# Moving most transposes of a fused LoRA MLP from TensorE to VectorE, and the mixing product to an earlier place

## The reference, cut to what matters

```python
x = x + conv(x) * mask                        # stage 0: long convolution by a state space kernel
x = x + einsum('bct,bcd->bdt', x, W1[cond])   # stages 1 and 2: a 32 x 32 matrix for each sample
x = x + einsum('bct,bcd->bdt', x, W2[cond])
# stage 3: gated MLP, H = 512, F = 1376, with one of 16 adapters (rank 16) for each sample
gate = x @ W_gate.T + 0.5 * (x @ A_gate[r].T) @ B_gate[r].T
up   = x @ W_up.T   + 0.5 * (x @ A_up[r].T)   @ B_up[r].T
act  = silu(gate) * up
x = x + act @ W_down.T + 0.5 * (act @ A_down[r].T) @ B_down[r].T
```

## Time and profile before

| | |
|---|---|
| median of 3 runs | 1069.36 us (1068.21 to 1069.70) |
| the profiled execution, its own time | 1069.72 us |
| its span, first to last instruction | 1067.9 us |
| TensorE busy, mean granted clock | 97%, 0.997 |
| VectorE, ScalarE, GpSimd busy | 46%, 38%, 45% |
| DMA engines busy (main queue) | 41.3% |

### The profile page before, as it was taken

The page is one execution under the profiler, slowest core; times in us unless marked ns, Lnnn a source line. Parts: engine busy times, 40 slices in busy tenths (PEclk is TensorE's granted clock), DMA queues, the critical chain, the costliest instruction groups (busy, mean ns, idle before and its releaser), DMA issues.

```text
span 1067.9 us, 19023 instructions
## 1 busy us (share of the span) xinstructions
PE 1037.9 (97%) x5922; PEld 906.3 (85%) x5922; DVE 490.4 (46%) x1095; ACT 402.1 (38%) x627; POOL 484.8 (45%) x301
## 2 busy tenths in 40 slices
PE   3999899999999999999999999999999999999998
PEld 3665688888898888888888988888888888888887
DVE  8333344545444445445454445454454444454442
ACT  7002234434433433344343334334443433443341
POOL 0605354545445444545454454445454544544441
PEclk9999899999999999999999999999999999999999
DMA  9799342424333343424243333434242433334320
GB/s 340 249 404 337 116 110 89 134 69 138 98 109 101 99 123 101 120 84 136 71 138 97 108 99 101 125 99 122 80 137 73 137 96 107 102 98 128 104 75 20
DMA packets 100980, 135.50 MB, mean 127 GB/s; under 512 B 26395, under 2 KB 59420, under 8 KB 100956
## 3 DMA queue, kind: packets, MB, share of 16 engines
q1 hardware_dynamic: 100380, 135.12, 41.3%
q10 hardware_dynamic: 576, 0.08, 0.1%
HBM read 118.11 MB, written 16.99 MB: 127 GB/s over the span
## 4 chain that ended last, share of the span: by engine, by line
PE 94%; DVE 3%; DMA 3%; issue 0%; ACT 0%; DVEq 0%; ACTq 0%
PE ps L984 47%; PE ps L1016 27%; PE ps L994 8%; PE ps L962 5%; PE ps L1005 4%; DMA x1p<-yo 2%; PE ps L1039 1%; PE ps L1038 1%; PE ps L975 1%; PE ps L972 1%; PE ps L973 1%; DVE x3r L815 0%; DMA tr<-kpad 0%; DVE xs L704 0%; PE ps L936 0%; PE ps L1027 0%
## 5 line engine op out<-in xcount | busy, mean ns | idle before, releaser
L984 PE MATMUL ps<-wg_hi,x_hi 128*128 128x512 f32 (+2 forms) x768 | 299.2, 390 | 4.6 <-DVE x_lo L805 4.6
L984 PE MATMUL ps<-wg_lo,x_hi 128*128 128x512 f32 (+2 forms) x768 | 291.7, 380 | 0.0
L984 PE MATMUL ps<-wg_hi,x_lo 128*128 128x512 f32 (+2 forms) x768 | 290.7, 379 | 0.0
L471 POOL TENSOR_TENSOR bst<-braw,bst 128x1024 fp32r<-128x1024 f32 (+1 forms) x96 | 212.7, 2215 | 90.7 <-ACT bst L572 90.7
L815 DVE STREAM_TRANSPOSE x3r<-x3n 32x128 f32<-32x128 f32 x512 | 155.0, 303 | 92.3 <-ACT x3n L545 85.8
L588 ACT ACTIVATE at_hi<-ps 128x512 fp32r<-128x512 f32 (+1 forms) x95 | 53.4, 562 | 315.1 <-PE ps L1005 315.1
L984 PEld LDWEIGHTS ps<-wg_hi,x_hi 128*128 128x128 f32 x768 | 145.1, 189 | 25.9 <-issue 4.7
L984 PEld LDWEIGHTS ps<-wg_hi,x_lo 128*128 128x128 f32 x768 | 145.1, 189 | 25.2
L984 PEld LDWEIGHTS ps<-wg_lo,x_hi 128*128 128x128 f32 x768 | 145.3, 189 | 20.4
L1016 PE MATMUL ps<-wd_hi,at_hi 128*128 128x288 f32 x696 | 151.9, 300 | 0.0
L1016 PE MATMUL ps<-wd_lo,at_hi 128*128 128x288 f32 x696 | 149.0, 296 | 0.0
(11 more groups left out here) (147 smaller groups left out, 1184.6 us busy)
## 6 DMA issues: line engine op xcount, KB each, us to landing
braw<-in_tb SPq DMA_DIRECT2D x256, 128.0 KB, 2.7
braw<-in_tb SPq DMA_DIRECT2D x128, 96.0 KB, 2.4
adraw<-in_tad SPq DMA_DIRECT2D x128, 88.0 KB, 1.9
tr<-kpad SPq DMA_DIRECT2D x16, 512.0 KB, 6.9
x1p<-yo SPq DMA_DIRECT2D x16, 512.0 KB, 5.7
xb<-in_x SPq DMA_DIRECT2D x32, 256.0 KB, 2.8
agraw<-in_ta SPq DMA_DIRECT2D x128, 64.0 KB, 2.0
bdraw<-in_tbd SPq DMA_DIRECT2D x128, 64.0 KB, 2.2
```

The lines of the kernel that those rows point to most:

```text
L471: sub(v, b_from(p, q), v.bitcast(F32), ALU.subtract).then_inc(s["blo"], 1)
L984: last = mm(bank[:, 0:n], x3s[a][:, k, :], wgs[b][:, k, o:o + n], start=(k == 0 and a + b == 0), stop=False, skip_group_check=True)
```

## The change

- VectorE makes the transposes of groups 1 and 2 (`a_turn` in the VectorE list, 16 instructions each, from `act_t` into `atp`). TensorE keeps those of group 0, and group 2 of the last tile.
- x3 is turned from a new SBUF copy `x3m` back into the PSUM bank `misc`, in two halves, and `x3_high` and `x3_low` read it there. A new ScalarE copy `x3_keep` saves x3 in `x3n` for the final sum. `x3r` goes away.
- On TensorE `mix(t + 1)` moves from behind `chunk(p, 2, 0)` to behind `chunk(p, 0, 1)`; `chunk(p, 1, 0)` moves ahead of `lora_b(t, p, 0)`, and `down` of group 2 behind it.
- `x` rows and mix weights are loaded for tile t + 2 in tile t; those of tile 1 are loaded ahead of the first block. The adapter loads for the next tile come first in `tile_io`. `x1_high` and `x1_low` come earlier in their lists.
- New semaphores: `atv` (VectorE turned a group), `dn` (`down` of group 0 or 1 is done), `x3k` (x3 saved).

```diff
 def x3_copy(t):                      # ScalarE
     act.wait_ge(s["x3mm"], t + 1)
-    copy(x3n[:, p, :], misc, ACT.Copy).then_inc(s["x3n"], 1)
+    copy(x3m[:], misc, ACT.Copy).then_inc(s["x3n"], 1)
+def x3_keep(t, p, free=None):
+    act.wait_ge(s["x3n"], t + 1)
+    if free is not None:
+        act.wait_ge(s["evac"], free)
+    copy(x3n[:, p, :], x3m[:], ACT.Copy).then_inc(s["x3k"], 1)
...
 def a_high(t, q, to=None):
-    act.wait_ge(s["att"], t * 3 + q + 1)
+    if q == 0:
+        act.wait_ge(s["att"], t + 1)
+    elif to is not None:
+        act.wait_ge(s["att"], NT + 1)
+    else:
+        act.wait_ge(s["dn"], t * 2 + q)
+        act.wait_ge(s["atv"], t * 2 + q)
...
+def turn(to, of, blocks):             # VectorE
+    for i, j in blocks:
+        rows, cols = slice(i * C, (i + 1) * C), slice(j * C, (j + 1) * C)
+        last = V.transpose(to[cols].rearrange("f (k n) -> f k n", n=P)[:, :, rows],
+                           of[rows].rearrange("n (k f) -> n k f", f=P)[:, :, cols])
+    return last
+GRID = [(i, j) for i in range(GB) for j in range(GB)]
+def x3_turn(t, part, done=False):
+    dve.wait_ge(s["x3n"], t + 1)
+    last = turn(misc, x3m[:], part)
+    if done:
+        last.then_inc(s["x3t"], 1)
+def a_turn(t, q):
+    dve.wait_ge(s["mul"], t * 3 + q + 1)
+    turn(atp, act_t[:], GRID).then_inc(s["atv"], 1)
...
 # tile_dve
 act_mul(t - 1, 1 - p, 2)
+a_turn(t - 1, 2)
 t_mask(t, p); t_turn(t); a_low(t - 1, 2); t_low(t)
-td_mask(t - 1, 1 - p); td_turn(t - 1)
+x3_turn(t + 1, GRID[0:8])
 act_mul(t, p, 0)
+x3_turn(t + 1, GRID[8:16], True)
+td_mask(t - 1, 1 - p); td_turn(t - 1)
+a_low(t, 0)
 td_low(t - 1)
-a_low(t, 0)
 out_sum(t - 1, ...)
 act_mul(t, p, 1)
-x3_turn(t + 1, 1 - p)
+a_turn(t, 1)
 a_low(t, 1); x3_low(t + 1)
...
 # tile_pe
 chunk(p, 0, 0)
-a_turn(t - 1, 2)
 chunk(p, 0, 1)
-down(t - 1, 1 - p, 2)
+mix(t + 1, 1 - p)
+pe.wait_ge(s["mul"], t * 3)
+chunk(p, 1, 0)
 lora_b(t, p, 0)
-chunk(p, 1, 0)
+down(t - 1, 1 - p, 2)
 a_turn(t, 0); chunk(p, 1, 1); lora_b_down(t - 1, 1 - p); lora_b(t, p, 1); chunk(p, 2, 0)
-mix(t + 1, 1 - p)
 down(t, p, 0)
-a_turn(t, 1)
 chunk(p, 2, 1); lora_b(t, p, 2); down(t, p, 1)
...
 # tile_act
 silu(t - 1, 1 - p, 2)
+x1_high(t + 1)
 a_high(t - 1, 2); t_high(t)
+x3_copy(t + 1)
 b_high(t, p, 1); silu(t, p, 0)
-td_high(t - 1); a_high(t, 0); ag_high(t + 1); x1_high(t + 1)
+ag_high(t + 1); a_high(t, 0); td_high(t - 1)
 b_high(t, p, 2); silu(t, p, 1); bd_high(t)
-x3_copy(t + 1, 1 - p); a_high(t, 1)
+x3_keep(t + 1, 1 - p)
 ad_high(t + 1); b_high(t + 1, 1 - p, 0)
+a_high(t, 1)
 x3_high(t + 1)
...
 # tile_io (SP queue)
-load_x(t + 1); load_b(t, here, p, 2)
-load_ag(t + 1); load_ad(t + 1); load_wbd(t, mixes, 1 - p); load_b(t + 1, there, 1 - p, 0)
+load_ag(t + 1); load_ad(t + 1); load_b(t, here, p, 2); load_b(t + 1, there, 1 - p, 0)
+mix_data(t + 2, mixes, p)             # load_x(t + 2), load_wbd(t + 2)
 store_out(t - 1); load_b(t + 1, there, 1 - p, 1); load_bd(t + 1)
```

More of the change, by code:

```diff
@@ L169, in cond_resid_kernel @@
         x3s = [sb("x3_hi", [P, KT, TN], F32R), sb("x3_lo", [P, KT, TN], F32R)]
-        x3r = sb("x3r", [P, T])
+        x3m = sb("x3m", [P, T])
         act_t = sb("act_t", [P, T])
@@ L185, in cond_resid_kernel @@
             ag aghi aglo ad adhi adlo b0 b1 bhi blo bd bdhi bdlo
-            bfree la tm tmt thi2 tlo2 gu silu mul att ahi alo td tdm tdt tdhi tdlo accd evac ost""".split() + [
+            bfree la tm tmt thi2 tlo2 x3k gu silu mul att atv dn ahi alo td tdm tdt tdhi tdlo accd evac ost""".split() + [
             f"wl{n}" for n in range(NW)] + [f"u{q}" for q in range(C // 2)]
@@ L338, in store_out, with mix_data @@
                 sp.dma_start(out[bass.ds(row, TN), :], outb[:]).then_inc(s["ost"], 16)
+            def mix_data(t, e, p):
+                load_x(t)
+                load_wbd(t - 1, e, p)
             def tile_io(t, p, here, there, mixes, first=False, last=False):
-                if not last:
-                    load_x(t + 1)
-                load_b(t, here, p, 2, t * 3 + 1)
                 if not last:
@@ L346, in tile_io @@
                     load_ad(t + 1, there)
-                    load_wbd(t if not first else None, mixes, 1 - p)
+                load_b(t, here, p, 2, t * 3 + 1)
+                if not last:
                     load_b(t + 1, there, 1 - p, 0, t * 3 + 2)
+                if mixes is not None:
+                    mix_data(t + 2, mixes, p)
                 if not first:
@@ L357, in block_io @@
                 there = None if last else entries(SP, i + 1, 0, NA, 0, GB)
-                mixes = entries(SP, i, 1, NCOND, GB, BB)
-                after = None if last else entries(SP, i + 1, 1, NCOND, 0, GB)
+                mixes = None if last else entries(SP, i + 1, 1, NCOND, 0, BB)
                 if first:
                     load_b(0, here[0:GB], 0, 1)
-                tile_io(i * 2, 0, here[0:GB], here[GB:], mixes, first=first)
-                tile_io(i * 2 + 1, 1, here[GB:], there, after, last=last)
+                tile_io(i * 2, 0, here[0:GB], here[GB:], None if last else mixes[0:GB], first=first)
+                tile_io(i * 2 + 1, 1, here[GB:], there, None if last else mixes[GB:], last=last)
             sp.wait_ge(s["kout"], 32)
@@ L423, in _ @@
             sp.wait_ge(s["yst1"], 16 * C // 4)
+            load_wbd(None, entries(SP, 0, 1, NCOND, GB, BB), 1)
+            load_x(1)
             block_io(0, first=True)
@@ L483, in tile_lows @@
                     x_sum(t + 1)
+                    x1_low(t + 1)
                 b_low(t, p, 1)
@@ L486, in tile_lows @@
                     ag_low(t + 1)
-                    x1_low(t + 1)
                 b_low(t, p, 2)
@@ L541, in x1_high, with x3_copy @@
                 copy(x1_hi[:], xa[:], ACT.Copy).then_inc(s["x1hi"], 1)
-            def x3_copy(t, p):
+            def x3_copy(t):
                 act.wait_ge(s["x3mm"], t + 1)
-                copy(x3n[:, p, :], misc, ACT.Copy).then_inc(s["x3n"], 1)
+                copy(x3m[:], misc, ACT.Copy).then_inc(s["x3n"], 1)
[4 more added lines that the diff above has]
+                copy(x3n[:, p, :], x3m[:], ACT.Copy).then_inc(s["x3k"], 1)
             def x3_high(t, free=None):
@@ L550, in x3_high @@
                     act.wait_ge(s["gu"], free)
-                copy(x3s[0][:].rearrange("p k n -> p (k n)"), x3r[:], ACT.Copy).then_inc(s["x3hi"], 1)
+                copy(x3s[0][:].rearrange("p k n -> p (k n)"), misc, ACT.Copy).then_inc(s["x3hi"], 1)
             def ag_high(t, first=False):
@@ L603, in _ @@
             act.wait_ge(s["yst1"], 16 * C // 4)
-            x3_copy(0, 0)
+            x3_copy(0)
             x3_high(0)
+            x3_keep(0, 0)
             act.wait_ge(s["msk"], 1)
@@ L611, in tile_act @@
                     silu(t - 1, 1 - p, 2)
+                if not last:
+                    x1_high(t + 1)
+                if not first:
                     a_high(t - 1, 2)
                 t_high(t)
+                if not last:
+                    x3_copy(t + 1)
                 b_high(t, p, 1, None if first else t * 3)
                 silu(t, p, 0)
+                if not last:
+                    ag_high(t + 1)
+                a_high(t, 0)
                 if not first:
                     td_high(t - 1)
[L618 to L621, removed]
                 b_high(t, p, 2, t * 3 + 1)
@@ L625, in tile_act @@
                 if not last:
-                    x3_copy(t + 1, 1 - p)
+                    x3_keep(t + 1, 1 - p, None if first else t)
+                    ad_high(t + 1, 1 - p, None if first else t)
+                    b_high(t + 1, 1 - p, 0, t * 3 + 2)
                 a_high(t, 1)
                 if not last:
-                    ad_high(t + 1, 1 - p, None if first else t)
-                    b_high(t + 1, 1 - p, 0, t * 3 + 2)
                     x3_high(t + 1, t * 3 + 3)
@@ L804, in x3_low @@
                 dve.wait_ge(s["x3hi"], t + 1)
-                tt(x3s[1][:].rearrange("p k n -> p (k n)"), x3r[:], x3s[0][:].rearrange("p k n -> p (k n)").bitcast(F32),
+                tt(x3s[1][:].rearrange("p k n -> p (k n)"), misc, x3s[0][:].rearrange("p k n -> p (k n)").bitcast(F32),
                    ALU.subtract).then_inc(s["x3lo"], 1)
-            def x3_turn(t, p):
-                dve.wait_ge(s["x3n"], t + 1)
[L811 to L816, removed]
+            def turn(to, of, blocks):
[6 more added lines that the diff above has]
+            def x3_turn(t, part, done=False):
+                dve.wait_ge(s["x3n"], t + 1)
+                last = turn(misc, x3m[:], part)
[4 more added lines that the diff above has]
+                turn(atp, act_t[:], GRID).then_inc(s["atv"], 1)
             def t_mask(t, p):
@@ L863, in out_sum @@
                 dve.wait_ge(s["accd"], t + 1)
+                dve.wait_ge(s["x3k"], t + 1)
                 if stored is not None:
@@ L875, in _ @@
             tt(x1_lo[:], xa[:], x1_hi[:].bitcast(F32), ALU.subtract).then_inc(s["x1lo"], 1)
-            x3_turn(0, 0)
```

(29 more changed lines are left out.)

## The result

The median went from 1069.31 us (4 executions, 1068.21 to 1069.70) to 1039.26 (4 executions, 1037.27 to 1040.91): ratio 0.972, interval 0.970 to 0.974. A ratio is the time over that of the kernel before; an interval is one of 95%. A later set of 5 on chip 0 gave 1038.70, ratio 0.970 (0.969 to 0.971). The forecast was 1036, its range 1031 to 1052.

A forecast was written before the change was run, and what follows sets the result against it. TensorE's instruction stream was taken as the bound, 29.40 us a tile. Savings of 33.0 in tiles 1 to 30 plus 0.88 in the last, less 0.6 in tile 0, made 33.3: 1036 us, range 1031 to 1052.

The forecast's parts named there:

- The path: TensorE, steady tiles: two groups of transposes at 0.44 us and a 0.22 us wait go, 1.10 a tile, 33.0 in all.
- The last tile's 0.88: TensorE, last tile: it loses its two groups of four transposes, 0.88 us; its tail stays as before.
- The price of a turn into PSUM: VectorE's transposes writing PSUM instead of SBUF: extra cost taken as 0, at most 0.133 us a turn.
- rival 1: VectorE turns into PSUM cost 0.054 to 0.10 us more each: 1043 us at 0.065, 1051 at 0.08; chance 0.12.
- the walk's tightest place: Rows laid end to end: group 1's low part ready at 24.2, due at TensorE's `down` at 25.1, 0.87 us to spare.
- The due times: Steady tile, all engines: each result for TensorE comes before it is wanted, so the tile takes 28.3 us.
- rival 2: VectorE's turns become the bound, over 0.10 us dearer each: 1117 us at 0.133; chance 0.08.
- Rival 3: The early `mix` on TensorE waits for its x: half a microsecond a tile gives 1052 us; chance 0.05.
- Rival 4: The transposes' time on TensorE comes back as other gaps, so nothing moves: 1069 us; chance 0.02.
- Tile 0: the mis-sized term: SP queue in tile 0: loads and index reads ahead of B delay it; charged 0.6 us, between 0 and 4.
- The median: Whole kernel: 1036.4 us from the profiled execution's 1069.72, taken as 1036 since the median was 0.4 lower.
- `x3_low`: VectorE subtraction: falls from 2.13 to about 0.69 us, taking an operand from PSUM.

The follow-up runs named there:

- Experiment 1: Changed kernel with group 1's four transposes back on TensorE, behind `down` of group 0: 1052.93 us, ratio 0.983 to the kernel before.
- experiment 2: Kernel before with the 16 turns of x3 cut in two halves, `a_low` of group 1 between them: 1064.26 us, ratio 0.994.
- experiment 3: Changed kernel with two or six further unused VectorE turns before those of group 1: 1046.78 us (ratio 0.980) and 1086.71 us (1.016).
- Experiment 8: Changed kernel with group 0's transposes on VectorE too, second half of x3's turns behind the final sum: 1130.15 us, ratio 1.055.
- experiment 5: Changed kernel with x and mix weights loaded one tile ahead again, at the head of a tile's loads: 1122.96 us, ratio 1.050.
- Experiment 6: Changed kernel with the loads around tile 0 reordered, B of groups 1 and 2 earlier: 1036.48 us and again 1036.37, ratio 0.967 both times.
- experiment 4: Changed kernel with x3 turned into an SBUF tensor instead of the PSUM bank `misc`: 1038.02 us, ratio 0.971.

## Why the prediction was right

**The path.** The step that carried the forecast, 1.10 us a tile from two groups of 0.44 and a wait of 0.22, measured 1.130. Experiment 1 put one of the groups back and found 0.440; experiment 2 took the wait out alone and found 0.217; the other group wasn't tested by itself. The last tile's 0.88 came out as 0.9.

**The price of a turn into PSUM.** Taken as 0, with 0.133 as the upper bound; it is 0.020. The page "Perfetto Trace Analysis" of the Trainium skill, section "Optimizing Scalar/DVE Operations", puts VectorE's access to PSUM (125 ns) 65 ns above that to SBUF (60 ns); the turns show 21 ns (0.324 against 0.303 us into SBUF in the kernel before). At 0.020 the price is below the 0.054 at which, by the prediction, it begins to count, so rival 1 didn't happen. Of the 0.87 us to spare 0.55 is left, and 16 × 0.020 is 0.32: the walk's tightest place was the right one. What it left out is that the weight loads want `at_lo` earlier: 0.39 of the 0.55 is free (experiment 3). So the price begins to count at about 0.044, an estimate by (0.87 − 0.16) / 16, and 0.020 is below that too.

**The due times.** No steady tile has a wait. Experiment 3 shows the cliff at the place that the walk named: past 0.39 us every added one counts (no dose below 0.61 was run). Experiment 8 gives rival 2 in another form: with 16 more turns the round through `td_low` and `lora_b_down` is the bound. Rival 3 came only with the late load of experiment 5. Rival 4 fell with the result, and experiment 1 shows that the transposes' time on TensorE counts in full.

**Tile 0: the mis-sized term.** It was charged 0.6 us and measured 2.6, and 0.3 ahead of it from the 16 dearer turns. The step was named (B of group 2 late by the loads and index reads put in front), and its bounds of 0 and 4 hold it. The walk had B of group 2 land at 137.7; it landed at 139.5. The four A issues behind the index reads took 3.55 us, against 1.99 in the kernel before, and the walk as recorded doesn't name the 1.3 us that ScalarE spends on a table load before its first silu (in both kernels). Experiment 6 gets 1.2 us back.

**The median.** 1036 against 1039.26. The 3.3 us are a sum in which errors partly cancel. Tile 0 and its lead cost 2.3 more than charged, the steady tiles gave 0.9 more than forecast (33.9 for 33.0): 1.4 by the profiled executions, 1037.8 against 1036.4. The other 1.9 us is how those executions lie to their medians, 0.4 above before and 1.5 below after. That the changed kernel's median lies higher comes from the two executions at 0.993; the trace of experiment 4 shows such a loss ahead of the steady tiles, and for these two it isn't shown.

**`x3_low`.** It was forecast at 0.69 and measured so. The prediction gave the operand in PSUM as the reason; in the new order GpSimd pauses then, which alone is enough (experiment 4), and the rows of `a_low` show that the operand would have been enough as well.

## What to carry to other kernels

When one engine's list is the time, work can be moved off it even to a slow helper: 32 turns of 0.336 us replaced eight transposes of 0.11 in each tile, and the transposes' 28 us were still won, because every result came before its due time. Lay the rows end to end and look for the smallest gap to a due time; that gap, not the helper's busy share, says how much more it can take. Then add a dose and measure it: the gap read was 0.55 us, the free part 0.39, with VectorE at 79%. And look at the first round by itself: loads put ahead of others are free in the steady loop and are paid once where the pipeline fills.

## What the runs showed of the hardware

A VectorE transpose of 32 × 128 float32 takes 0.303 us into SBUF and 0.324 into PSUM. A VectorE subtraction of 128 × 512 with both operands in SBUF took 0.693 us with GpSimd idle and 2.13 beside a GpSimd subtraction; with one operand in PSUM it took 0.69 either way. This agrees with the Trainium skill, "SBUF — State Buffer", section "Who interferes with whom", by which a VectorE instruction with two inputs in SBUF contends with a GpSimd instruction that reads SBUF. A wait of TensorE of 3.3 us every other tile cost more than its length: the clock granted in that stretch fell to 0.95. And executions of nearly the same program reach tile 0 2 to 4 us apart where the clock granted before it differs (0.91 or 1.00 in 70 to 90 us), while their steady tiles agree to 0.002 us.
